# Pieces of 128 elements for VectorE beside indirect scatters, and new cells ranked inside their scatter pass

## The reference

```python
x = x + L0(h)   # mixture of 6 gaussians of the edge's coordinates, mean over dst, plus h @ root
x = x + L1(h)   # two mean aggregations with 32 -> 64 -> 32 (SAGE)
x = x + L2(h)   # spline convolution; see below
x = x + L3(h)   # two sum aggregations with 32 -> 64 -> 32 (SAGE)
```

```python
basis, idx = spline_basis(pseudo)                  # [E, 8] weights and matrix numbers
h = elu(spline_conv(ones,   ..., stn1_w)); h = elu(spline_conv(h, ..., stn2_w))
t = (elu(h @ stn3_w + b)) @ stn4_w + b
new_pseudo = clip(pseudo + t[col] - t[row], 0, 1)  # new coordinates: new cells
basis2, idx2 = spline_basis(new_pseudo)
out = spline_conv(x, ..., basis2, idx2, conv_w)    # sum over row, divided by the degree
```

## Time and profile before

| | us |
|---|---|
| median of 3 runs | 10544.22 |
| lowest and highest | 10543.03, 10548.49 |
| the profiled execution's own time | 10548.12 |
| its span in the profile | 10546.3 |
| busy in it: PE, DVE, ACT, POOL | 6169.8, 5914.7, 2150.7, 6510.9 |

### The profile page before, as it was taken

One profiled execution on the slowest core, in us unless ns is written; L12 is line 12 of the kernel. 1 busy time (PEld: TensorE's weight loads), 2 busy tenths in 40 slices (PEclk: granted clock), 3 DMA queues, 4 the chain that ended last, 5 costly groups with the idle time before them and its releaser, 6 DMA issues. The chain is left out here.

```text
span 10546.3 us, 181138 instructions
## 1 busy us (share of the span) xinstructions
PE 6169.8 (59%) x49368; PEld 5217.4 (49%) x49369; DVE 5914.7 (56%) x12028; ACT 2150.7 (20%) x5870; POOL 6510.9 (62%) x6754
## 2 busy tenths in 40 slices
PE   5552056666677776666556566645554555555565
PEld 5442035555677764444444555334444444445554
DVE  8993076555566658888695645731111333367645
ACT  0000024444333331111103140011111111124140
POOL 3777727777677776777443146357777777765140
PEclk9999987887555558888656575665555555557575
DMA  6993012222433321111285656682000111125655
GB/s 212 303 117 26 5 50 85 84 85 77 112 104 104 104 84 47 54 54 53 53 186 177 155 212 166 139 59 27 14 14 9 28 28 28 28 44 207 143 217 119
DMA packets 1315177, 1004.33 MB, mean 95 GB/s; under 512 B 894007, under 2 KB 1157419, under 8 KB 1306047
## 3 DMA queue, kind: packets, MB, share of 16 engines
q1 hardware_dynamic: 954526, 648.46, 26.7%
q0 software_dynamic: 225216, 279.29, 8.5%
q10 hardware_dynamic: 135264, 74.60, 3.1%
HBM read 495.63 MB, written 546.44 MB: 99 GB/s over the span
## 5 line engine op out<-in xcount | busy, mean ns | idle before, releaser
L2823 POOL DMA_INDIRECT msg<-msg,idx x1792 | 1743.2, 973 | 593.1 <-issue 528.6
L1166 POOL DMA_INDIRECT run_rows<-rec,idx x544 | 598.9, 1101 | 1108.3 <-ACT rec L1144 979.6
L2653 POOL DMA_INDIRECT cell<-rec,idx x944 | 936.5, 992 | 509.9 <-issue 284.1
L2373 POOL DMA_INDIRECT cell<-rec,idx x944 | 971.6, 1029 | 334.5 <-issue 286.7
L2034 POOL DMA_INDIRECT rec_d<-rec,idx x880 | 881.6, 1002 | 452.2 <-issue 267.1
L511 POOL DMA_INDIRECT rec_r<-sc_rec,sc_idx x832 | 885.7, 1065 | 431.7 <-issue 286.4
L2803 PE MATMUL ps<-w_stn,hft 128*128 x1792 | 599.1, 493 | 405.0 <-ACT hft L2757 401.9
L2590 PE MATMUL ps<-h_rows,oht 128*128 x1888 | 450.9, 403 | 547.3 <-ACT oht L2597 546.8
L826 DVE TENSOR_TENSOR oh<-iota_f,rd 128x512 f32<-128x512 f32 x237 | 167.3, 708 | 1023.1 <-PE ps L2575 1022.4
L2590 PEld LDWEIGHTS ps<-h_rows,oht 128*128 128x128 f32 x1888 | 420.3, 328 | 640.8 <-issue 640.8
L2803 PE MATMUL ps<-w_conv,hft 128*128 x1792 | 438.4, 426 | 499.8 <-ACT hft L2757 499.8
(11 more groups left out here) (455 smaller groups left out, 15787.6 us busy)
## 6 DMA issues: line engine op xcount, KB each, us to landing
loc<-loc_s SPq DMA_DIRECT2D x68, 2048.0 KB
got<-run_rows SPq DMA_DIRECT2D x472, 224.0 KB
got<-rec_d SPq DMA_DIRECT2D x236, 416.0 KB
rec_d<-padd SPq DMA_DIRECT2D x4, 12480.0 KB
...
loc<-loc_d ACTq DMA_DIRECT2D x118, 256.0 KB
```

Of the source, the lines that this page charges most:

```text
L1166: nc.gpsimd.indirect_dma_start(out=out, out_offset=bass.IndirectOffsetOnAxis(ap=idx[:, u, m % HU:m % HU + 1], axis=0), in_=rec[:, m, :], i ...
L2373: nc.gpsimd.indirect_dma_start(out=cells, out_offset=bass.IndirectOffsetOnAxis(ap=idx[:, n, g:g + 1], axis=0), in_=rec[:, n, g, :], in_off ...
L2653: nc.gpsimd.indirect_dma_start(out=cells, out_offset=bass.IndirectOffsetOnAxis(ap=idx[:, n, g:g + 1], axis=0), in_=rec[:, n, g, :], in_off ...
L2823: nc.gpsimd.indirect_dma_start(out=msgs, out_offset=bass.IndirectOffsetOnAxis(ap=idx[:, n, g:g + 1], axis=0), in_=msg[:, n, g, :], in_offs ...
```

## The change

Three things are changed.

(a) Operations of VectorE with two operands, beside scatters, are cut into pieces. `hots_by_tile` makes a one-hot of 4 x 128 elements by four instructions of 128 in stages 3, 4 and 9 (other uses of `one_hot` stay whole). `rank_hot` and the product in `rank_position` come in pieces of 128 elements, the gaussians' two operations of 720 elements in stage 3 in four of 180, and the comparison of 1024 bf16 elements in `send_runs` in two of 512. The semaphore is raised by the last piece.

(b) `place_cells` becomes `count_cells`. It only counts, by `tally_marks` and `tally_pe` (eight matmuls of one column per bin, with weights of 118 columns, on TensorE), and the layer norm's instructions stand between the bins. The second pass over 64 bins is gone. `to_cells` ranks each batch with `rank_hot`, `rank_batch` and `rank_position`, as stage 2 does, makes the row numbers itself (`index`), and POOL waits for them (`s_idx`) as well.

(c) `cell2` is blanked in stage 6, on ACT's queue behind `run_rows`.

```diff
+            s = dict(bank=bank, upto=upto, J=J, parts=[slice(g, g + 2 // J) for g in range(0, G, 2 // J)])
...
         def rank_hot(v, s, key, k, m):
+            shape = [P, s["J"], G // len(s["parts"]), CELLS]
             v.wait_ge(s["s_rank"], k + 1)
-            nc.vector.tensor_tensor(s["hot"][:, m, :, :, :], bcast(iota_f[:, 0:CELLS].unsqueeze(1).unsqueeze(1), shape),
-                                    bcast(key.unsqueeze(3), shape), ALU.is_equal).then_inc(s["s_hot"], 1)
+            for B in s["parts"]:
+                made = nc.vector.tensor_tensor(s["hot"][:, m, :, B, :], bcast(iota_f[:, 0:CELLS].unsqueeze(1).unsqueeze(1), shape),
+                                               bcast(key[:, :, B].unsqueeze(3), shape), ALU.is_equal)
+            made.then_inc(s["s_hot"], 1)
...
-            nc.vector.tensor_tensor(sel, sel, s["hot"][:, m, :, :, :], ALU.mult).then_inc(s["s_sel"], 1)
+            for B in s["parts"]:
+                taken = nc.vector.tensor_tensor(sel[:, :, B, :], sel[:, :, B, :], s["hot"][:, m, :, B, :], ALU.mult)
+            taken.then_inc(s["s_sel"], 1)
...
+        def hots_by_tile(oh, local):
+            for g in range(G):
+                made = nc.vector.tensor_tensor(oh[:, g, :], iota_f[:, :], bcast(local[:, g:g + 1], [P, P]), ALU.is_equal)
+            return made
...
                                 for w in range(SUPER):
-                                    made = nc.vector.tensor_scalar(hot[:, m % RING, w, :], loc[:, u, m % HU, :], lane_c[:, w:w + 1], None,
-                                                                   ALU.is_equal)
+                                    for e in (slice(0, HR * P), slice(HR * P, RUN * P)):
+                                        made = nc.vector.tensor_scalar(hot[:, m % RING, w, e], loc[:, u, m % HU, e], lane_c[:, w:w + 1], None,
+                                                                       ALU.is_equal)
...
                     turn_hot(k + 1, (n + 1) % R)
+                    rank_batch(pe, ranks, k, n)
                     ids = block_ids(ENG.PE, "d", t, NB - 1)
...
+                        def index(i, k, t, n, first):
+                            rank_position(v, ranks, pos[:, :].unsqueeze(1), k, n)
+                            v.wait_ge(ranks["s_pos"], k + 1)
+                            nc.vector.tensor_tensor(pos_i[:, :], pos[:, :], rd[:, ds(t, G), ATT], ALU.add).then_inc(s_row, 1)
+                            v.wait_ge(s_row, 3 * k + 1)
+                            nc.vector.tensor_scalar(lane[:, :], pos_i[:, :], P - 1, None, ALU.bitwise_and).then_inc(s_row, 1)
+                            nc.vector.tensor_scalar(tile[:, :], pos_i[:, :], 7, None, ALU.arith_shift_right).then_inc(s_row, 1)
+                            v.wait_ge(s_row, 3 * k + 3)
+                            if not first:
+                                v.wait_ge(sent[n], 16 * G * i)
+                            nc.vector.scalar_tensor_tensor(out=idx[:, n, :], in0=lane[:, :], scalar=float(TC), in1=tile[:, :],
+                                                           op0=ALU.mult, op1=ALU.add).then_inc(s_idx, 1)
+
+                        def turn(i, first):
+                            for n in range(R):
+                                k, t = i * R + n, i * STEP + n * G
+                                pick_hot(v, s, k + 1, t + G, (n + 1) % R)
+                                rank_hot(v, ranks, rd[:, ds(t + G, G), ROWC].unsqueeze(1), k + 1, (n + 1) % R)
+                                index(i, k, t, n, first)
...
-                                nc.scalar.copy(idx[:, n, :], rd[:, ds(t, G), ROWC])
...
                                 pool.wait_ge(filled, i * R + n + 1 + R)
+                                pool.wait_ge(s_idx, i * R + n + 1)
...
-                blank = ((run_rows, zpad[:, 0:RUNW], TILES_D),)
+                blank = ((run_rows, zpad[:, 0:RUNW], TILES_D), (cell2, pad2[:, :, :].rearrange("p u w -> p (u w)"), TC))
```

More of the change, by code:

```diff
@@ L379, in tally_marks @@
         def tally_marks(v, c, key, bins):
-            for b in range(bins):
+            for b in bins:
                 if b >= 4:
@@ L2565, in pick_rings, with pick_pe @@
             return s
-        def pick_pe(pe, s, nodes, W, pitch, out_free):
+        def pick_pe(pe, s, nodes, W, pitch, out_free, ranks):
             def turn_hot(k, n):
@@ L2600, in pick_hot, with to_cells @@
             v.wait_ge(s["turned"], k + 1)
-            one_hot(s["oh"][:, n, :, :], rd, t, LOC).then_inc(s["hot"], 1)
-        def to_cells(nodes, pitch, F, cells, load_weights, blank):
+            hots_by_tile(s["oh"][:, n, :, :], rd[:, ds(t, G), LOC]).then_inc(s["hot"], 1)
+        def to_cells(nodes, pitch, F, cells, load_weights, blank, base):
             W = F + 4
@@ L2609, in to_cells @@
                 s_w = sem_in(c, "weights")
+                ranks = rank_rings(c, 4, base)
+                pos, pos_i, lane, tile = (sb_in(c, n, [P, G], dt) for n, dt in (("pos", F32), ("pos_i", I32), ("lane", I32), ("tile", I32)))
+                s_row, s_idx = (sem_in(c, n) for n in ("row", "indexed"))
                 filled, s_blank = sem_in(c, "filled"), sem_in(c, "blanked")
@@ L2619, in _ @@
                     def _(v):
+                        def index(i, k, t, n, first):
[16 more added lines that the diff above has]
+                                index(i, k, t, n, first)
                         pick_hot(v, s, 0, 0, 0)
-                        with v.Fori(0, NID) as i:
-                            for n in range(R):
-                                pick_hot(v, s, i * R + n + 1, i * STEP + (n + 1) * G, (n + 1) % R)
+                        rank_hot(v, ranks, rd[:, 0:G, ROWC].unsqueeze(1), 0, 0)
+                        turns(v, NID, turn)
                     @block.tensor
@@ L2828, in _, with count_cells @@
                             pool.wait_ge(sent[n], 16 * G * NIC)
-        def place_cells(blank):
+        def count_cells(base, h_nm):
             T = slice(0, TILES_D)
             with ExitStack() as c:
-                w = sort_own(c, sort_shared(c, TILES_D))
+                w = tally_own(c, tally_shared(c, TILES_D), 0)
                 i0, key, key_b = sb_in(c, "i0", [P, TILES_D, KD]), sb_in(c, "key", [P, TILES_D]), sb_in(c, "key_b", [P, TILES_D], BF16)
-                k, s_blank = sem_in(c, "chain"), sem_in(c, "blanked")
+                d, sq = sb_in(c, "d", [P, NB, C]), sb_in(c, "sq", [P, NB, C])
+                m, var, std, r = (sb_in(c, n, [P, NB]) for n in ("m", "var", "std", "r"))
+                k, s_var, s_std, s_h = (sem_in(c, n) for n in ("chain", "var", "std", "h"))
                 with nc.Block() as block:
@@ L2844, in _ @@
                     def _(act):
-                        blank_tables(act, s_blank, blank)
+                        act.wait_ge(s_var, 1)
+                        nc.scalar.activation(std[:, :], var[:, :], ACT.Sqrt).then_inc(s_std, 1)
                     @block.tensor
                     def _(pe):
-                        sort_pe(pe, w, CELLS)
+                        tally_pe(pe, w, CELLS)
                     @block.vector
@@ L2853, in _, with marks @@
                         then = chain(v, k)
-                        sort_consts(then, w)
+                        def marks(b0, b1):
+                            tally_marks(v, w, key_b[:, :], range(b0, b1))
                         new = rd[:, T, NEWP:NEWP + KD]
@@ L2923, in build @@
         with ExitStack() as c:
-            place_cells(((cell2, pad2[:, :, :].rearrange("p u w -> p (u w)"), TC),))
-            next_phase()
+            base = sb_in(c, "cell_base", [P, 1, CELLS])
             h_nm = sb_in(c, "h_rows", [P, NB, C + 1])
-            layer_norm(None, h_nm)
+            count_cells(base, h_nm)
             w_sb = sb_in(c, "w_conv", [P, WS * F2])
```

58 lines of the change are left out of this document (43 added, 15 removed).

## The result

| | before | changed |
|---|---|---|
| median, us | 10543.62 (4 runs) | 10474.11 (4 runs) |
| lowest and highest | 10540.60, 10548.49 | 10470.58, 10495.74 |
| ratio, with its 95% interval | | 0.9935, 0.9919 to 0.9950 |
| span of the profiled execution | 10546.3 | 10471.0 |

A forecast was written before the change was run, and what follows sets the result against it. POOL's indirect DMAs, issued one after another, were taken to bound the scatter stages. Terms: -50 - 13 - 36 - 35 - 114 + 28 + 68 = -152, from 10548.1 to 10396, median 10393; range 10300 to 10500.

The forecast's parts named there:

- send_runs: The four stages with send_runs: comparison cut in two halves POOL's 70 us of stalls, -35 us (-50 to 0).
- F: Rival: pieces don't let POOL in, or stalls multiply with their number; half the pieces' gain is left, 10460; chance 0.07.
- Stage 4: Of 54 us of POOL's stalls, uncut products make some 5; the pieces give -36 us (-42 to -20).
- Stage 2: Of 77 us of POOL's stalls, 69 come from the two cut operations; 19 kept, -50 us (-60 to -30).
- Stage 3: Of 26 us of POOL's stalls, half by cut operations, three quarters of those gone: -13 us (-20 to -5).
- place_cells and layer norm: Second pass and layer norm's block removed, counting slightly longer: -114 us (-125 to -95).
- The blanking: Blanking cell2 in stage 6: some 60 of its 90 us hidden, the stage waits for the rest, +28 us (0 to +45).
- to_cells: New loop between VectorE and TensorE takes 5.5 us per batch, above POOL's 5.1: +68 us (-17 to +162).
- B: Rival: the loop in to_cells is no longer than POOL's batch; -17 in place of +68, 10308; chance 0.18.
- C: Rival: the loop in to_cells takes 5.8 to 6.1 us, +140 to +210 there, 10465 to 10535; chance 0.12.
- D: Rival: slower than before, the loop in to_cells above 6.15 us; at 6.5, +304, 10628; chance 0.04.
- E: Rival: two-operand instructions don't bar POOL and its stalls stay; only -35 of the pieces' -134 left, 10492; chance 0.03.

The follow-up runs named there:

- e8b: The changed kernel, but stage 2 compares and multiplies 512 elements in one instruction again, on a usual chip: 10514.9 us, ratio 0.9971.
- a0: The changed kernel as it is, measured again later: 10441.9 us, ratio 0.9913.
- e3: The changed kernel, but in to_cells TensorE ranks batch k ahead of the transposes of batch k+1: 10380.4 us, ratio 0.9845.
- e8: The changed kernel, but stage 2 compares and multiplies 512 elements in one instruction again, on the chip of late transfers: 12722 us.
- e5 to e8: The changed kernel with, in turn: stage 4's one-hot whole; its products halved; send_runs paced by POOL; stage 2 whole. Chip of late transfers: 12644 to 12763 us.

## Why the prediction missed

It named the direction, and the time lies in its range, but less than half of the forecast gain came, and the time is above the forecast's own 10345 to 10450. By its steps:

- **send_runs, the step that failed.** "VectorE's four pieces at 0.20 are 0.8 us per set, as now, under POOL's 1.4." The 0.20 is a row of 128 elements of f32, and the pieces have 512 of bf16: they cost 0.264 each, 1.05 per set, and VectorE ran on behind TensorE without waiting for it. With it failed "So a stall lasts at most one instruction, and its mean falls with the instruction's length": one DMA was held through 72 pieces. The trace of before spoke against that already, with two DMAs of 4.05 us in `send_runs`. +43 in place of -35 is 78 us, as much as the whole miss of 77; that the rest comes to nothing is luck, since stage 4's 30 too few are made up by 20 in the blanking and 18 in `to_cells`. Its upper bound of 0 was too low. I had a rival of this kind (F, 0.07), whose 10460 is nearest to the time, but worked it out as a half of (a) at every stage and not as this one with its condition: VectorE's work per set against TensorE's. Half of the 43 us is the long DMAs; why POOL is also idle 21 us longer stays open.
- **Stage 4.** -6 for -36. The stalls at the one-hot did fall to a fifth (49 to 9 us). I took the uncut products at "some 5" of 54 as they were; released from the shield they took 40. That the engines run in step was said, and used only as a reason to keep less.
- **Stage 2.** Right: -49 in the first profile, and 56 of POOL's time between e8b and a0. **Stage 3.** -8 for -13, within its bounds.
- **place_cells and layer norm.** -112.9 for -114. The counting takes as long as forecast: 90.9 us to the first scatter, 90 forecast.
- **The blanking.** +8 for +28. I took only "some 60 of its 90 us" as done beside the loads. The queue's rows and the windows of that stretch show all of it issued by 5483, 13 us before the stage's end, with VectorE busy for 85 and 95% of the two windows, where it was for 100% in the earlier trace rows. The prediction took the loads' 0.37 of the DMA engines off what the blanking can use; with both at work the share is 1.14 and 1.19:

```profile
5172.30 204.63 ACTq L533 DMA_DIRECT2D run_rows<-zpad  x8
5392.82 90.16 ACTq L533 DMA_DIRECT2D cell<-pad  x8
```

```profile
5373.00:5430.00 57.00, 28.11 (x474) 26.05 (x475) 48.20 (x112) 0.00 (x0) 0.00 (x0) 0.65 1.14 267
5430.00:5480.00 50.00, 26.35 (x443) 24.09 (x440) 47.56 (x111) 0.00 (x0) 0.00 (x0) 0.64 1.19 258
```

- **to_cells.** +50 for +68: mechanism right (e3 removes it), and the loop 5.43 us in the mean where 5.5 was worked out. The granted clock stayed at 0.50 there.

Of the rivals, B, C and D are out, and so is E: the same instructions, whole or in pieces, change POOL's excess in stage 2 from 77.8 to 22.2 us (e8b and a0). The Trainium skill (page "SBUF — State Buffer", section "Who interferes with whom") says, as an inference, that `tensor_tensor` does not stall descriptor generation; e8b does not bear that out. The same section also says that an instruction of VectorE with two inputs in SBUF contends with a GpSimd instruction that reads SBUF, and one with at most one such input, outside the modes with two ports, does not. The stalls fit that (46 of 48 at L440, 1 of 50 at L436) if POOL's DMA counts as a reader, its row numbers `idx` being in SBUF, which no run here tests; the prediction left that sentence out. It further says that `tensor_scalar` can enter a mode with two ports and that the port pair is an exclusive lock held for the whole instruction; the 19.76 us fit that, but it does not say that a chain of them can keep POOL out for 72 in a row (18.9 us at 0.262).

What stays open: why instructions of 1024 elements, twelve of them without a pause from 5675.42 on, held the DMA at 5677.53 for 0.30 us only (in the kernel before, 203 of the 260 holds reached into two such instructions, 55 into one and 2 into nine), and 96 of 512 held one for 18.8. Both leave nearly the same overlap between one and the next, 0.085 and 0.08 us. And where the edits of the changed kernel lost their 2 to 3% on the chip of late transfers was not tried: no trace of the kernel before was taken there. In e8 `to_cells` took 1710 us there, against 1284 in e8b, and POOL waited 578.4 us for `DVE idx`.

## What to carry to other kernels

Cutting VectorE's instructions helped POOL's indirect DMAs only where VectorE could not run ahead of POOL: count its work per batch with the pieces against the engine that paced it before, and if it is no longer held back, tie it to POOL (here by a semaphore, six sets deep, which kept every DMA under 4.1 us). A stall is also a shield: ask what stands at the place where the released instruction will come next. And when ranks, positions or the like are moved into a scatter pass, let TensorE do them ahead of the next batch's transposes, so that no engine waits for an answer that hangs on its own next output.

## What the runs showed of the chip

- An indirect DMA on POOL that comes into a running chain of VectorE's bf16 comparisons of 512 elements can be shut out until the chain ends: 19.76 us here, until 0.84 us after the last piece, and 19.74 to 19.77 in six of the seven profiles of the changed `send_runs` on the usual chips. Once in step, POOL gets in once per DMA through an unbroken chain, at 0.97 us, and every fourth piece lasts 0.575 us in place of 0.342.
- In stage 2 an f32 operation with both operands in SBUF held 46 of 48 DMAs, one with an operand in PSUM 1 of 50, a reduction none of 62. POOL loses where VectorE's instruction is at least 0.18 us old when the DMA is 0.126 us old (173 of 173), and wins at 0.17 us or less (14 of 14).
- Halving f32 products from 192 to 96 elements (start to start 0.268 and 0.168 us) raised the mean stall from 0.215 to 0.278 us.
- A bf16 comparison costs VectorE 0.40 us from start to start at 1024 elements and 0.26 at 512: 0.13 of it does not shrink.
- One chip took 12355 us for the kernel that takes 10539 on the others, and e5 to e8 took 12644 to 12763 on it, 2.4 to 3.3% longer than the kernel before: a verdict on such a change can turn with the chip. That the late transfers are the reason was not tested.
